# Two unit streams on TensorE: one first-layer chunk and one second-layer chunk in turn

## The reference

```
out = 0
for e in range(8):                        # Silu / Gelu / Relu, hidden width 512 / 512 / 256
    h = act(xt @ W1[e] + b1[e]) @ W2[e] + b2[e]
    out = out + h * score[:, e:e + 1]     # score: top 2 of the router, zero elsewhere
L2 conv: pooled mean -> offsets -> clipped positions -> 3-tap samples -> x * sigmoid(gate)
L3 conv: alpha = mean(x); fm = relu(sum_c(x * alpha) * w); out = 1 - wf * sigmoid(scale * thresholded fm)
```

## Time and profile before

| | |
|---|---|
| median of 3 executions | 437.06 us (433.48, 437.06, 438.8) |
| profiled execution, its own time | 433.28 us |
| its span, first to last instruction | 431.5 us |
| mean granted TensorE clock | 0.985 |
| TensorE busy | 387.8 us, 90% of the span |
| ScalarE busy | 279.1 us, 65% |
| VectorE busy | 257.9 us, 60% |
| GpSimd busy | 158.7 us, 37% |
| mixtures, from 149.05 us to the last matmul at 425.35 us | 276.3 us |

### The profile page before, as it was taken

The page is one execution under the profiler, slowest core; times in us unless marked ns, Lnnn a source line. Parts: engine busy times, 40 slices in busy tenths (PEclk is TensorE's granted clock), DMA queues, the critical chain, the costliest instruction groups (busy, mean ns, idle before and its releaser), DMA issues.

```text
span 431.5 us, 4941 instructions
## 1 busy us (share of the span) xinstructions
PE 387.8 (90%) x1589; PEld 274.6 (64%) x1591; DVE 257.9 (60%) x554; ACT 279.1 (65%) x502; POOL 158.7 (37%) x130
## 2 busy tenths in 40 slices
PE   7999969888999899999899969799897998878983
PEld 2467646443646678887687747577665777547762
DVE  1744235884341877665676784754846756577665
ACT  5131225855111967776987967779869889778762
POOL 3900000550084507423685662111115454333243
PEclk9999999999999899999999999899999999999998
DMA  8930000000000005752110003342031100421162
GB/s 285 431 114 0 0 2 0 1 2 0 0 2 0 1 24 149 298 155 78 34 46 4 0 4 106 62 134 89 0 99 51 33 18 0 99 74 26 21 157 70
DMA packets 29298, 28.75 MB, mean 67 GB/s; under 512 B 1127, under 2 KB 27047, under 8 KB 29016
## 3 DMA queue, kind: packets, MB, share of 16 engines
q1 hardware_dynamic: 29272, 28.43, 21.7%
HBM read 27.81 MB, written 0.62 MB: 66 GB/s over the span
## 4 chain that ended last, share of the span: by engine, by line
PE 53%; ACT 20%; DVE 18%; issue 5%; DMA 3%; POOL 1%; POOLq 0%; DVEq 0%; ACTq 0%; SPq 0%
PE ps L401 11%; PE ps L403 11%; PE ps L402 11%; ACT hidh L927 6%; ACT ps L928 6%; PE ps L408 3%; DVE hidl L1246 3%; DMA scores_all<-rows_scratch 3%; PE ps L639 2%; PE ps L413 2%; ACT rstd L835 2%; DVE parts L1256 2%; PE ps L585 1%; DVE bot L1168 1%; ACT L983 1%
## 5 line engine op out<-in xcount | busy, mean ns | idle before, releaser
L1246 DVE TENSOR_TENSOR hidl<-ps,hidh 128x512 fp32r<-128x512 f32 x160 | 108.5, 688 | 76.9 <-ACT ps L928 76.2
L372 POOL TENSOR_TENSOR x<-x,parts 128x512 f32<-128x512 f32 x47 | 60.7, 1291 | 161.9 <-DVE parts L1256 111.8
L927 ACT ACTIVATE hidh<-ps,par 128x512 fp32r<-128x512 f32 x96 | 67.5, 704 | 26.0 <-PE ps L403 25.7
L401 PE MATMUL ps<-xh,wh_all 128*128 128x512 f32 x160 | 69.6, 435 | 5.9 <-DVE hidl L1246 5.0
L401 PE MATMUL ps<-hidh,wh_all 128*128 128x512 f32 (+1 forms) x162 | 67.9, 419 | 5.1 <-DVE hidl L1246 4.0
L928 ACT ACTIVATE ps<-ps,par 128x512 f32<-128x512 f32 x96 | 65.1, 678 | 0.0
L403 PE MATMUL ps<-xl,wh_all 128*128 128x512 f32 x160 | 64.3, 402 | 0.0
L402 PE MATMUL ps<-xh,wl_all 128*128 128x512 f32 x160 | 64.0, 400 | 0.0
L402 PE MATMUL ps<-hidh,wl_all 128*128 128x512 f32 (+1 forms) x162 | 62.9, 388 | 0.0
L403 PE MATMUL ps<-hidl,wh_all 128*128 128x512 f32 (+1 forms) x162 | 62.9, 388 | 0.0
L365 POOL TENSOR_TENSOR wl_all<-wa,wh_all 128x512 fp32r<-128x512 f32 x40 | 50.9, 1290 | 3.5
(11 more groups left out here) (228 smaller groups left out, 571.6 us busy)
## 6 DMA issues: line engine op xcount, KB each, us to landing
scores_all<-rows_scratch SPq DMA_DIRECT2D x48, 256.0 KB, 5.0
wa<-in_moe SPq DMA_DIRECT2D x2, 4096.0 KB, 15.8
wa<-in_moe SPq DMA_DIRECT2D x1, 2048.0 KB, 11.5
dft_x<-in_dft_x SPq DMA_DIRECT2D x1, 640.0 KB
dft_o<-in_dft_o SPq DMA_DIRECT2D x1, 640.0 KB
w<-in_w_bottom SPq DMA_DIRECT2D x1, 576.0 KB, 7.1
w<-in_w_out SPq DMA_DIRECT2D x1, 576.0 KB, 8.8
cst<-in_consts SPq DMA_DIRECT2D x1, 512.5 KB, 7.9
```

The source lines that it names most:

```text
L372: pool.tensor_tensor(half(x, h), half(x, h), parts[:, n % 2, :], ALU.add).then_inc(s["state_added"], 1)
L401: pe.matmul(o, wh, xhi, start=start, stop=False)
L927: act.activation(hidh[:, n % 2, f, :], sums, func, bias=bias).then_inc(s["hidden_hi_act"], 1)
L1246: dve.tensor_tensor(hidl[:, n % 2, f, :], bank(sums_bank(n, f)), f32(hidh[:, n % 2, f, :]), ALU.subtract).then_inc(s["hidden_lo"], 1)
```

## The change

1. TensorE's order in the mixtures: for each pair of units, chunk 0 of `front(n + 1)`, chunk 0 of `back(n)`, chunk 1 of `front(n + 1)`, chunk 1 of `back(n)`, and so on, in two halves (`first_half`, `second_half`); at the step from 4 chunks to 2, one front chunk before two back chunks. Preparation steps of TensorE may now stand between the two halves of a unit. The number of matmuls in the units is the same.
2. Preparation steps placed anew on all engines, mostly one to three units earlier in the block. The routing of block nx ends inside the block before: `turn_route(nx)` in the middle of its last unit (`j == 6` in block 3), `keep_rows(nx)` soon after. `positions` and `hats` are each cut in two, `route_end` in four.
3. `scale(n - 1)` stands before `low(n, last chunk)` instead of after it.
4. The last unit of blocks 0 to 3 is added to the state by VectorE itself (`ends_half`), GpSimd only waits for it.
5. `rows` is laid out as (8, 1024): `turn_route` makes four transposes of 8 rows instead of one of 32, `keep_rows` copies 8x512 instead of 32x128, and the score loads read 2 KB runs instead of four of 512 B.
6. `offset_inputs` and `saliency_inputs` lose a small instruction each.

```diff
-                sp.dma_start(dram["rows"][m, 4 * h:4 * h + 4, :].rearrange("t (e p) -> (t e) p", e=E),
-                             rows[:, h * C:(h + 1) * C]).then_inc(s["rows_stored"], 16)
+                sp.dma_start(dram["rows"][m][:, h * HALF:(h + 1) * HALF], half(rows, h)).then_inc(s["rows_stored"], 16)
...
-                    sp.dma_start(scores_all[:, slot, :].rearrange("c (t p) -> c t p", p=C), ...
+                    sp.dma_start(scores_all[:, slot, :], dram["rows"][m, e:e + 1, h * HALF:(h + 1) * HALF]
+                                 .to_broadcast([C, HALF])).then_inc(s[f"scores{slot}_in"], 16)
...
             def add_part(n):
+                if ends_half(n):                      # n % E == E - 1 and n < 4 * E
+                    pool.wait_ge(s["state_added"], n + 1)
+                    return
...
-                pe.transpose(bank(6 if kb < 2 else 7, WIDE, C), wgt[:, WIDE * h:WIDE * (h + 1)], ident).then_inc(...)
+                for t in range(4):
+                    last = pe.transpose(bank(6 if kb < 2 else 7, E, C, t * C), wgt[:, (4 * h + t) * E:(4 * h + t + 1) * E], ident)
+                last.then_inc(s["route_turned"], 1)
...
+            def first_half(n):
+                if widths(n) == widths(n + 1):
+                    for f in range(widths(n) // 2):
+                        front(n + 1, (f,))
+                        back(n, (f,))
+                else:
+                    front(n + 1, (0,))
+                    back(n, (0, 1))
+            def second_half(n):                       # the same for the other chunks
...
             for kb in (1, 2):                         # TensorE, as it is now
                 for j in range(E):
                     first_half(kb * E + j)
                     j == 0: center(4, hh)   j == 4: variance(5, hh)   j == 5: logits(nx)   j == 7: turn_route(nx)
                     second_half(kb * E + j)
                     j == 0: variance(4, hh) j == 1: offsets(hh)       j == 2: deform(hh)   j == 3: center(5, hh)
             for j in range(E):                        # block 3
                 mid:   j == 0: center(6, 0)   j == 3: variance(7, 0)  j == 4: logits(4)    j == 6: turn_route(4)
                 after: j == 0: variance(6, 0) j == 1: saliency(0)     j == 2: center(7, 0)
             for j in range(E):                        # block 4
                 mid:   j == 1: variance(6, 1) j == 4: variance(7, 1)  j == 5: logits(5)    j == 7: turn_route(5)
                 after: j == 0: center(6, 1)   j == 2: saliency(1)     j == 3: center(7, 1)
...
             for j in range(1, E + 1):                 # VectorE, blocks 1 and 2, as it is now
                 f == 3: scale(n - 1) before low(n, 3)
                 after low: (1,3) norm_half(4), pool_sums, offset_inputs   (2,0) deform_inputs   (2,1) positions(hh, 0)
                 (2,2) positions(hh, 1)   (3,1) gate_half   (5,1) norm_half(5)   (5,2) norm_low(5)   (5,3) route_start
                 (6,0) route_pick   (6,2) route_exps   (6,3) route_softmax   (7,0) route_two   (7,1) route_shares   (8,1) keep_rows
             # ScalarE: (1,1) square(4)   (1,3) inverse_root(4)   (2,3) hats(0)   (3,0) hats(1)   (3,1) gate_tanh
             #          (4,3) square(5)   (5,1) inverse_root(5)   (5,2) high_part   (6,1) route_tanh
             # block 4, VectorE: (2,1) norm_half(6, 1), pool_sums, saliency_inputs, then scale, then low
             #          (3,1) scale, threshold, add_rest, low, saliency_half   (5,1) norm_half(7, 1)
             #          (6,1) scale, norm_low, low, route_start, route_pick   (7,0) route_end   (8,0) keep_rows
             # block 4, ScalarE: (2,0) inverse_root(6, 1)   (3,0) rectify   (3,1) saliency_tanh   (4,1) square(7, 1)
             #          (5,0) table load, inverse_root(7, 1)   (5,1) high_part   (6,1) route_exp
+                if ends_half(n):                      # at the end of scale(n)
+                    state = half(x, n // E % 2)
+                    dve.wait_ge(s["scaled"], n + 1)
+                    dve.wait_ge(s["state_added"], n)
+                    dve.tensor_tensor(state, state, parts[:, n % 2, :], ALU.add).then_inc(s["state_added"], 1)
```

More of the change, by code:

```diff
@@ L698, in back @@
                                start=(f == 0), stop=(f == q_n - 1))
-                last.then_inc(s["part_sums"], 1)
+                    if f == q_n - 1:
+                        last.then_inc(s["part_sums"], 1)
+            def first_half(n):
[7 more added lines that the diff above has]
+            def second_half(n):
+                if widths(n) == widths(n + 1):
+                    for f in range(widths(n) // 2, widths(n)):
+                        front(n + 1, (f,))
+                        back(n, (f,))
+                else:
+                    front(n + 1, (1,))
+                    back(n, (2, 3))
             def last_back():
@@ L748, in _ @@
             for n in range(E):
-                front(n + 1)
-                back(n)
+                first_half(n)
+                second_half(n)
                 if n == 0:
@@ L807, in _ @@
                     variance(7, 1)
-                back(4 * E + j)
+                elif j == 5:
+                    logits(5)
+                elif j == 7:
+                    turn_route(5)
+                second_half(4 * E + j)
                 if j == 0:
@@ L814, in _ @@
                     center(7, 1)
-                elif j == 5:
-                    logits(5)
             for j in range(E - 1):
-                front(5 * E + j + 1)
-                if j == 0:
-                    turn_route(5)
-                back(5 * E + j)
+                first_half(5 * E + j)
+                second_half(5 * E + j)
             last_back()
@@ L1435, in _ @@
                         elif (j, f) == (7, 0):
[L1436 removed]
+                            route_two(nx)
                         elif (j, f) == (7, 1):
[L1438 to L1452 removed]
+                            route_shares(nx)
+                        elif (j, f) == (8, 1):
+                            keep_rows(nx)
```

332 lines of the change are left out of this document (173 added, 159 removed).

## The result

| | kernel before | changed kernel |
|---|---|---|
| first comparison, median | 436.87 us (433.48 to 438.8) | 421.48 us (418.57 to 428.76) |
| ratio | | 0.963, interval 0.954 to 0.973 |
| repeated comparison, median | 438.76 us | 422.52 us (418.43 to 427.87) |
| ratio | | 0.964, interval 0.958 to 0.970 |

The change makes the kernel 3.6% faster. The profile that came with the first comparison is of an execution of 428.76 us in which parts ran at a lower clock, so the ratios leave such executions out and the rows here are those of the same kernel in the repeated comparison, an execution of 418.57 us with a span of 416.8.

The account below looks back on a forecast made before the run. TensorE's queue order was the bound: 23.6 idle + 2.9 drains + 1.7 half clock = 28.2 us at most. With 13.1 left, 15.1 gained less 2.0 for transposes, rounded to 14: 419.3 profiled, 421 median, range 409 to 437.

Parts of the forecast that it names:

- The likeliest case: Whole kernel: 421 us at the median, own range 415 to 428, chance 0.50.
- the drains: TensorE's pipeline emptying behind stops in the mixtures: 0.17 us for each of 17 shown waits, 2.9 us to gain.
- the transposes: TensorE's routing turns: four transposes for one cost 0.4 us at each of five turns, 2.0 us (bounds 0 and 3).
- The four waits of units 33 to 40: TensorE late for low(34, 1) 1.4 us, center(7, 1) 0.9, logits(5) 2.6, hidden(39, 0) 2.1; with small rest 7.9 left.
- The term of 1.7 us for the earlier trace: Block 2, ahead of the offsets: six matmuls at 1.2 GHz behind a 2.19 us stop take 3.13 us instead of 1.39.
- Layer 3's smaller slack: Units with two chunks: alternating, the second layer's chunk is wanted 3.48 us after the first-layer one, slack 0.6 instead of 1.3.
- Alternating adds and removes nothing.: TensorE's order in the units: no matmul added or removed, eight turns a unit instead of two cost nothing; only slack changes.
- my theories for the two parts: Placement removes most waits and alternation adds slack, or even spacing does most; either part alone no slower than the kernel before.
- (a): Whole kernel: everything hidden, only the transposes and some 3 us stay, gain 23, 410 to 414 us; chance 0.15.
- (b): Long blocks and layer 3: waits change place, passing on to `hidden`; gain about 7, 429 to 436 us; chance 0.22.
- (c): TensorE's clock falls behind short stops as frequent as one per unit: 35 us lost against 14, 458 us; chance 0.08.
- (d): Whole kernel: removed waits were not limiting because ScalarE sets the pace anyway, 433 to 438 us; chance 0.05.

Follow-up runs that it names:

- the second try: Changed kernel with whole front and back only for n = 2, block 4's steps reordered, low(34, 1) ahead of saliency_inputs and scale(33) among them: 417.35 us, ratio 0.953.
- the rows experiment: Changed kernel with the old row layout (one transpose, 32x128 copy, score loads in 512 B runs): 426.17 us, ratio 0.976, against 422.52 with the new layout.

## Why the prediction was right, point by point

**The whole.** 421 us were forecast, 421.48 measured; for the profiled execution 419.3 against 418.57. The gain in the mixtures was 14.6 us for 14. The likeliest case held, but some of its terms were off in both directions, and that the total came out to 1 us is in part luck: the idle time left was put 3.7 us too high, the drains 1.4 us too high as a gain, the transposes 0.4 us too high, and 0.9 us was added by rounding. The mixtures of the first profile, at a clock of 0.91 in units 33 to 40, took 265.06 us, a gain of 11.2 only. In the medians 15.4 and 16.2 us were measured, for the 16 that 421 stands for; the 2 us beyond the 14 came from taking 421 between 419.3 and 423, not from a term.

**The idle time that stays.** Forecast 0.3, 0.8, 1.5, 1.8, 7.9, 0.8 us; measured 1.20, 0.93, 0.00, 0.55, 5.84, 0.92. The four waits of units 33 to 40 were foreseen one by one: 1.4, 0.9, 2.6 and 2.1 us forecast, 1.24, 0.90, 2.24 and 1.38 measured. The second shows as the second-layer matmul at 368.95, which waits for `low(35, 1)` and stands ahead of `center(7, 1)`. In units 9 to 32 the walk through the queues overrated what is late, by 2.6 us. That units 9 to 16 came out near the forecast is luck in part: of their 0.8 us, 0.5 were to stand behind the two `positions` around unit 10, and nothing stops there; both stops (0.21 and 0.67 us) are ahead of first-layer chunks of units 15 and 16, by the routing, where 0.3 us was forecast. In units 17 to 24 ScalarE at 94% did not stop TensorE once, and their 52.48 us lie just under the 53 to 55 that were to show the forecast right. Why the late steps did no more harm, no run shows; that they overlap is the prediction's own guess.

**The step that failed: units 1 to 8.** I said that the gap shrinks to 0.3 us. I saw that `front(1)` and `back(0)` share a wait, and did not look at the part bank: alternating, unit 2's first second-layer chunk begins 2.1 us earlier (0.70 us after the unit instead of 2.78), and its bank is free only after `scale(0)`, which needs the first score load. The stretch grew from 45.70 to 46.89 us where it was to shrink by 0.4: the stop of 0.70 us is gone, one of 1.20 has come, and two transposed routings add 0.66. With the old rows the same wait is 3.48 us, so the layout, which I had priced only as 2.0 us of cost in the stream and a shorter load in block 5, pays for itself in unit 2 instead. By the counts from the table load the start lost 1.1 us, and the second try shows that it need not have.

**Transposes and loads.** Four transposes took 0.44 us where one took 0.12, five times: 1.6 us in all for the 2.0 forecast (0.33 per stretch in the rows experiment). A sixth, in units 33 to 40, shows no effect (35.42 us with one transpose, 35.41 with four). The load is 3.4 us for 2.9 forecast, nearer to that end than to 5.5, and the row copy 0.67 us for 0.69. In block 5 both are early enough, as said.

**Drains and the half clock.** The term of 1.7 us for the earlier trace rows is gone with its stop. The 2.9 us of drains was too much: I counted 17 waits of 20 and let all of them go, while 11 stay, so 9 x 0.17 = 1.5 us can go. With these terms the sum is 14.1 idle + 1.7 + 1.5 - 1.6 = 15.7 us, for 14.6; the busy time fell by 0.45 us where the last three make 1.6, and no row shows where that 1.1 us is.

**Layer 3's smaller slack.** I put its slack at 0.6 us alternating for 1.3 whole. No run shows a price for it: with whole fronts the two stretches take 35.43 and 22.32 us, alternating 35.41 and 22.42, and the stops are nearly the same. The four waits in units 33 to 40 are those of the placement.

**"Alternating adds and removes nothing."** For TensorE's stream alone that held: between turns the matmuls stay 0.232 us apart (units 17 to 24: no idle time, 52.48 us). As a statement about the change it misled. I priced the parts one after the other as if they added. They don't: the mixtures take 276.3 us before, 299.2 with the alternation alone, 287.5 with the placement alone, 261.7 with both, in one profile each. Alone they cost 4.2 and 2.4%; the placement is made for the later third and fourth chunk, the alternation needs steps moved ahead of it. Both of my theories for the two parts fell. The runs show that in units 1 to 32 neither part is worth anything alone, while in layer 3 the placement alone does it all. That single steps have a place for one order only was tried for two of them, `square` and `scale`, at 3 us each; for the others it is an argument.

**Rivals.** (a) All hidden, 410 to 414: units 33 to 40 speak against it, as said, but the mended kernel's 417.35 shows that a part of it was to be had. (b) Waits that change place: right for each part alone, wrong for both together. (c) The clock: it did fall behind short stops, to 0.50 behind 1.43 and 0.89 us in the placement alone, and in the first profile of the changed kernel, where units 33 to 40 took 37.27 us at a clock of 0.91 and 35.41 at 1.00 in the repeated one. It cost some 2 us there, not what would give 458 us. The Trainium skill, TensorE: Matmul & The Clock Gate, section A second HAM failure mode: psum-queue depth-cycling, has the clock swing in a kernel that cycles through PSUM banks with short idle times between its groups of matmuls. Here the five banks in turn alone did not bring such swings: the clock is 1.00 in all six windows, with 9.4 us of idle time in them. The falls looked at here came behind stops. (d) ScalarE-bound: excluded by the stretch without idle time at 94% of ScalarE.

## What to carry to other kernels

When two streams are interleaved more finely, each producer's last piece moves later in the unit and each consumer's first piece moves earlier; everything queued behind or ahead of those on the other engines has to be looked at for the new order, and both halves of such a change are to be costed together, since each alone can lose. Walk also through the first units, where operands come from a cold chain (rows, store, load), and ask of every buffer, PSUM banks included, who asks for it earlier than before. Before two versions of a first stretch are compared, check that they start alike: count from an event that both share, as the table load here. What a stop costs is more than its length, because short stops can bring the clock to its lower level; so removing the last few can be worth more than their sum.

## What was not expected of the hardware

- A matmul behind a stop costs more than its share: the one at 162.81 us has a row of 0.50 us and is followed after 0.34 instead of 0.23 us, so 0.11 us on top of the idle time.
- The clock's fall behind stops of 1 to 2.2 us is not the same in each execution: behind the stop of 2.24 us ahead of the logits, units 33 to 40 took 37.27 us (clock 0.91) in one execution and 35.41 us (1.00) in another. In the profiled executions of all these kernels unit 1 begins anywhere from 149 to 156 us.
- A lower clock just ahead of a wait can cost nothing there: with `front(0)` in part at 1.2 GHz (clock 0.58 in the 4 us ahead of unit 1 in the changed kernel's profile) unit 1 starts 1.6 us later behind the table load, and unit 9 at the same distance from it, 52.14 us against 52.04 and 51.94.
- A 256 KB load in 2 KB runs took 3.4 us, in 512 B runs 5.2 us in the changed kernel with the old rows and 5.0 in the kernel before (medians of 48).
- With all state adds on GpSimd instead of four on VectorE, the only effect on a stretch is 0.65 us in units 17 to 24. The Trainium skill, SBUF — State Buffer, section Who interferes with whom, has the two engines block each other. The trace agrees for one add of four, with both inputs in SBUF: it took 1.70 us instead of 0.69 and ended 0.56 us after GpSimd's two splitting steps did (249.27 + 2.55 = 251.82). It was ready 0.16 us before the centering asked for it, so no run here shows a cost on the path.
